# Rounding the experts' hidden layer: VectorE or ScalarE, with a second buffer

## The reference

```python
x = x + 0.5 * ffn(layernorm(x))
x = x + attn(layernorm(x))
x = x + 0.5 * ffn(layernorm(x))
```

## Time and profile before

| | |
|---|---|
| median of 3 runs | 596.25 us |
| the profiled execution | 595.64 us |
| its span, first to last instruction | 593.8 us |
| TensorE busy | 523.8 us (88%) |
| VectorE busy | 424.1 us (71%) |
| ScalarE busy | 215.2 us (36%) |
| GpSimd busy | 138.3 us (23%) |
| mean granted TensorE clock | 0.968 of full speed |

### The profile page before, as it was taken

One profiled execution on the slowest core, in us unless ns is written; L12 is line 12 of the kernel. 1 busy time (PEld: TensorE's weight loads), 2 busy tenths in 40 slices (PEclk: granted clock), 3 DMA queues, 4 the chain that ended last, 5 costly groups with the idle time before them and its releaser, 6 DMA issues.

```text
span 593.8 us, 7881 instructions
## 1 busy us (share of the span) xinstructions
PE 523.8 (88%) x2796; PEld 378.9 (64%) x2820; DVE 424.1 (71%) x796; ACT 215.2 (36%) x351; POOL 138.3 (23%) x131
## 2 busy tenths in 40 slices
PE   0485879999999999999999999999999656799997
PEld 0483556666676666758666676766667653577776
DVE  3759886986975686697476688735785777997742
ACT  0125633432624222271422254232221026665540
POOL 3140012354001324401323410132330100321220
PEclk9995989999999999999999999999999996999999
DMA  8995004000101000000200001030117940013112
GB/s 280 372 413 227 1 1 161 1 1 0 36 18 55 35 1 1 1 37 18 88 0 0 0 0 53 1 124 1 54 54 286 383 171 11 1 54 124 37 54 88
DMA packets 16607, 48.14 MB, mean 81 GB/s; under 512 B 1600, under 2 KB 1856, under 8 KB 15296
## 3 DMA queue, kind: packets, MB, share of 16 engines
q1 hardware_dynamic: 15760, 47.19, 21.3%
q10 hardware_dynamic: 816, 0.54, 0.5%
HBM read 39.33 MB, written 8.39 MB: 80 GB/s over the span
## 4 chain that ended last, share of the span: by engine, by line
PE 58%; DVE 15%; issue 13%; POOL 5%; DMA 3%; SPq 3%; ACT 2%; DVEq 0%; ACTq 0%; POOLq 0%
PE bank L382 8%; PE bank L635 8%; PE bank L642 8%; PE bank L384 8%; PE bank L383 8%; PE bank L636 7%; DMA route_w<-in_switch_w 3%; POOL rs L998 3%; SPq L408 2%; PE bank L600 2%; DVE h_lo L1194 2%; PE bank L514 2%; PE bank L486 1%; PE bank L532 1%; DVE h_hi L1193 1%
## 5 line engine op out<-in xcount | busy, mean ns | idle before, releaser
L635 PE MATMUL bank<-xh,win_hi 128*128 128x512 f32 x304 | 136.7, 450 | 0.0
L636 PE MATMUL bank<-xl,win_hi 128*128 128x512 f32 x304 | 119.5, 393 | 0.0
L642 PE MATMUL bank<-xbf,win_lo 128*128 128x512 bf16 x296 | 79.6, 384 | 1.7 <-issue 0.2
L998 POOL TENSOR_TENSOR rs<-ms,neg_half 128x16 f32<-128x16 f32 x16 | 49.2, 3077 | 129.0 <-ACT ms L843 129.0
L635 PEld LDWEIGHTS bank<-xh,win_hi 128*128 128x128 f32 x304 | 57.5, 189 | 17.4 <-issue 0.3
L636 PEld LDWEIGHTS bank<-xl,win_hi 128*128 128x128 f32 x304 | 57.3, 189 | 10.5
L985 POOL TENSOR_TENSOR xa<-xa,b_half 128x512 f32<-128x512 f32 x28 | 40.1, 1446 | 64.5 <-DVE z_lo L1212 32.1
L382 PE MATMUL bank<-w_hi,z_hi 128*128 128x512 f32 x128 | 51.6, 403 | 0.0
L642 PEld LDWEIGHTS bank<-xbf,win_lo 128*128 128x128 bf16 x320 | 25.0, 98 | 41.3 <-issue 22.7
L384 PE MATMUL bank<-w_hi,z_lo 128*128 128x512 f32 x128 | 50.0, 391 | 0.0
L383 PE MATMUL bank<-w_lo,z_hi 128*128 128x512 f32 x128 | 49.9, 390 | 0.0
(11 more groups left out here) (175 smaller groups left out, 1045.3 us busy)
## 6 DMA issues: line engine op xcount, KB each, us to landing
route_w<-in_switch_w SPq DMA_DIRECT2D x4, 2048.0 KB, 14.2
route_w<-in_switch_w SPq DMA_DIRECT2D x16, 512.0 KB, 16.3
raw<-in_w_in SPq DMA_DIRECT2D x4, 1280.0 KB, 18.7
xa<-in_x SPq DMA_DIRECT2D x4, 1024.0 KB, 6.6
out<-x SPq DMA_DIRECT2D x16, 256.0 KB, 2.0
x_dram<-x1p SPq DMA_DIRECT2D x12, 256.0 KB, 2.0
xa<-x_dram SPq DMA_DIRECT2D x3, 1024.0 KB, 5.6
x_chunk<-in_x SPq DMA_DIRECT2D x2, 1024.0 KB, 23.4
```

The source lines that it names most:

```text
L635: pe.matmul(bank[:], win_hi[:, c, r, k, :], xh[:, k, :], start=(k == 0), stop=False)
L636: pe.matmul(bank[:], win_hi[:, c, r, k, :], xl[:, k, :], start=False, stop=False)
L642: mm = pe.matmul(bank[:], win_lo[:, c, r, k, :], xbf[:, k, :], start=False, stop=(k == KC - 1))
L998: pool.tensor_tensor(rs[:], ms[:], neg_half[:], ALU.pow).then_inc(s_rs, 1)
```

## The change

The row ends (feed-forwards 1 to 3) get a second pair `h_hi2`, `h_lo2` for odd chunks. It lies in memory over `decay`, `qt`, `q_sq` and `yt`, which the attention is done with by then; the first write to it waits for the last y_lo. A chunk's rounding now waits for the O two chunks back. ScalarE rounds expert 0, between the two GELUs, and VectorE rounds expert 1. In phase 0 ScalarE rounds both experts, still with one pair, so that it waits for the O just before; for chunk 0 it waits for VectorE's second `select`. VectorE's split of w3 moves from between the splits of chunks 0 and 1 to behind `z_split(0, 0)`. TensorE's order and the late phase stay.

```diff
+        with ExitStack() as region:
+            h_hi2 = sb("h_hi2", [P, TOPK, S], F32R, into=region)
+            h_lo2 = sb("h_lo2", [P, TOPK, S], F32R, into=region)
         decay = sb("decay", [P, S])
...
+        hid2 = (hf, h_hi2, h_lo2)
...
         def hid_set(f, c):
-            return hid1 if is_late(f) and c % 2 else hid0
+            if is_late(f):
+                return hid1 if c % 2 else hid0
+
+            return hid0 if is_first(f) or c % 2 == 0 else hid2
...
+        def hid_reader(f, c):
+
+            if is_first(f):
+                return job_first(f"O{c - 1}") if c >= 1 else None
+            return job_row(f - 1, f"O{c - 2}") if c >= 2 else None
...
+            def hidden_act(f, c):
+
+                _, hi, _ = hid_set(f, c)
+                for k in range(TOPK):
+                    gelu(f, c, (k,))
+                    if k == 0 or is_first(f):
+                        reader = hid_reader(f, c)
+                        if reader is not None:
+                            act.wait_ge(s_ob, reader + 1)
+                        elif c == 1:
+                            act.wait_ge(s_yl, KC * f)
+                        else:
+                            act.wait_ge(s_sel[1], f + 1)
+                        act.wait_ge(s_gelu, H_JOBS * f + TOPK * c + k + 1)
+                        act.activation(hi[:, k, :], hf[:, k, :], ACT.Copy).then_inc(s_hh0, 1)
...
-                gelu(f, 0)
+                hidden_act(f, 0)
                 t1_out(f, 3)
-                gelu(f, 1)
+                hidden_act(f, 1)
                 for c in range(KC):
                     z_out(f, c)
                     if c < 2:
-                        gelu(f, c + 2)
+                        hidden_act(f, c + 2)
...
-                gelu(0, 0)
-                gelu(0, 1)
+                hidden_act(0, 0)
+                hidden_act(0, 1)
...
-            def split_hidden(f, c, read_job):
+            def split_hidden(f, c):
 
                 src, hi, lo = hid_set(f, c)
                 for k in range(TOPK):
-                    ve.wait_ge(s_gelu, H_JOBS * f + TOPK * c + k + 1)
-                    if k == 0 and read_job is not None:
-                        ve.wait_ge(s_ob, read_job + 1)
-                    own.do(ve.tensor_copy(hi[:, k, :], src[:, k, :]))
+                    if k == 0 or is_first(f):
+                        ve.wait_ge(s_hh0, hi_count(f, c, k))
+                    else:
+                        ve.wait_ge(s_gelu, H_JOBS * f + TOPK * c + k + 1)
+                        reader = hid_reader(f, c)
+                        if reader is not None:
+                            ve.wait_ge(s_ob, reader + 1)
+                        own.do(ve.tensor_copy(hi[:, k, :], src[:, k, :]))
                     ve.tensor_tensor(lo[:, k, :], src[:, k, :], hi[:, k, :], ALU.subtract).then_inc(s_hl, 1)
...
-            split_hidden(0, 0, None)
-            ve.wait_ge(s_w3h, 1)
-            ve.scalar_tensor_tensor(out=w3_lo[:], in0=w3_raw[:], scalar=0.5, in1=w3_hi[:], op0=ALU.mult,
-                                    op1=ALU.subtract).then_inc(s_w3l, 1)
+            split_hidden(0, 0)
             for c in range(KC):
-                job = job_first(f"O{c}")
                 if c < KC - 1:
-                    split_hidden(0, c + 1, job)
+                    split_hidden(0, c + 1)
                 z_split(0, c, x_bank[c])
+                if c == 0:
+                    ve.wait_ge(s_w3h, 1)
+                    ve.scalar_tensor_tensor(out=w3_lo[:], in0=w3_raw[:], scalar=0.5, in1=w3_hi[:], op0=ALU.mult,
+                                            op1=ALU.subtract).then_inc(s_w3l, 1)
```

More of the change, by code:

```diff
@@ L222, in macaron_kernel, with is_first @@
         hid1 = (hf1, h_hi1, h_lo1)
+        hid2 = (hf, h_hi2, h_lo2)
         first_chunk = [xa, x1p, x_chunk2, x_chunk3]
+        def is_first(f):
+            return isinstance(f, int) and f == 0
         def is_late(f):
@@ L293, in macaron_kernel @@
         s_hh = sem("s_hh")
+        s_hh0 = sem("s_hh0")
         s_hl = sem("s_hl")
@@ L360, in job_ffn, with hi_count @@
             return job_first(name) if isinstance(f, int) and f == 0 else job_row(f - 1, name)
+        def hid_reader(f, c):
+            if is_first(f):
+                return job_first(f"O{c - 1}") if c >= 1 else None
+            return job_row(f - 1, f"O{c - 2}") if c >= 2 else None
+        def hi_count(f, c, k):
+            return PAIR * c + k + 1 if is_first(f) else H_JOBS + KC * (f - 1) + c + 1
         def job_late(f, name):
@@ L772, in t1_out, with gelu @@
                 act.activation(use["xt_hi"][:, c, :], x_bank[c][:], ACT.Copy).then_inc(s_t1e, 1)
-            def gelu(f, c):
+            def gelu(f, c, ks=range(TOPK)):
                 if c == 0:
                     act.wait_ge(s_b1, f + 1)
-                for k in range(TOPK):
+                for k in ks:
                     act.wait_ge(s_h, H_JOBS * f + TOPK * c + k + 1)
@@ L890, in first_ffn @@
                     if c < 2:
-                        gelu(0, c + 2)
+                        hidden_act(0, c + 2)
             table_loads()
@@ L1351, in row @@
                         if n < KC - 1:
-                            split_hidden(b + 1, n + 1, job)
+                            split_hidden(b + 1, n + 1)
                         if n == 0:
@@ L1363, in row @@
                         if n == 0:
-                            split_hidden(b + 1, 0, None)
+                            split_hidden(b + 1, 0)
                         if n == 1:
@@ L1427, in _ @@
                 w3_add(2 * B - 1, t, job_late(2 * B - 1, f"W{t}"), out_bank(f"W{t}"))
-VE_ROW_STEPS = 60
+VE_ROW_STEPS = 56
 def kernel(**inputs):
```

## The result

The changed kernel took 598.87 us (median of 7 runs, 598.75 to 603.93), the kernel before in the same session 595.72 us. The ratio is 1.0066, 95% interval 1.0049 to 1.0083: slower, by 3.15 us in the medians where 2.5 was forecast. The profiled execution took 598.80 us. First its page: the span, the busy shares and the chain by engine.

A forecast was written before the change was run, and what follows sets the result against it. VectorE's load was taken as the main limit in the row ends, with ScalarE's copy late instead after the change. Phase 0 +3.1 and rows -0.6 give +2.5 on 596.25: 598.8 us, eight in ten runs from 596.9 to 601.3.

The forecast's parts named there:

- Likeliest case: Whole kernel: phase 0 costs +3.1 us, row ends give -0.6, so slower by 2.5 at 598.8 us; chance 0.56.
- step O1 to O2: Phase 0, step (5): from O1's end to O2's end takes 3.90 us, where it was 3.34, +0.56.
- step O2 to O3: Phase 0, step (6): from O2's end to O3's takes 3.68 us, where it was 3.34, +0.34.
- split of w3 moved: Phase 0: VectorE's split in its new place delays h_lo of (2,0) and O2; cost 0.15 us, bounds 0 and 1.05.
- own wait of ScalarE: Row ends: ScalarE's copy waits for its own preceding GELU, taken as 0.05 us, ends 0 and 0.17.
- gain per row end: Row ends: O2's last matmul starts at 265.41 instead of 265.61, -0.2 us each, -0.6 for three.
- (1): Phase 0: copy of (0,0) waits for VectorE's second select, GELU (0,1) queues behind; `hidden` 1 at 55.05 instead of 53.21, +1.84.
- (3): Phase 0: copy of (1,0) waits for O0 and holds up GELU (1,1); `hidden` 2 at 60.80 instead of 57.86.
- Relief whole: Rival for the row ends: copy off the path, VectorE's 1.84 us per row end won in full; 593.9 us, chance 0.05.
- Absorbed: Rival: a later wait shrinks by half of phase 0's delay or more; 595.7 to 597.2 us, chance 0.14.
- Dear own wait: Rival: ScalarE's own wait is 0.17, rows give +0.5 and phase 0 +0.6; 600.5 us, chance 0.07.
- Late clock: Rival in phase 0: idle gap behind O0, `hidden` 2 and O1 run at low clock, 1.8 us more; 600.6, chance 0.18.

The follow-up runs named there:

- experiment 1: Only the row ends changed against the kernel before (second buffer pair, ScalarE rounds expert 0 between the GELUs), phase 0 as before: 595.28 us, ratio 0.9991.
- experiment 4: Against experiment 1, ScalarE rounds expert 1 behind its GELU and VectorE expert 0 in the row ends: 591.41 us, ratio 0.9927.
- Experiment 8: Against experiment 1, ScalarE's copy of expert 0 stands behind both GELUs in the row ends: 595.23 us, ratio 0.9992.
- experiment 12: Against Experiment 8, VectorE and TensorE take expert 1 first in the row ends, GELUs wait in that order: 593.69 us, ratio 0.9974.
- experiment 5: Against the changed kernel, two buffer pairs in phase 0 too, odd chunks' pair where the routing weights were: 595.50 us, ratio 0.9999.
- experiment 11: Against experiment 5, even chunks take the pair where the routing weights were, so the first copy skips the select wait: 594.05 us, ratio 0.9967.
- its control: The changed kernel run again without any edit: 599.64 us over 6 runs, ratio 1.0089.
- experiment 6: Against experiment 4, phase 0 also gets two buffer pairs with ScalarE rounding expert 1 there: 589.76 us, ratio 0.9896.
- experiment 2: Only phase 0 changed against the kernel before (ScalarE rounds both experts, one pair, split of w3 moved), row ends as before: 599.42 us, ratio 1.0086.
- experiment 7: Against the changed kernel, VectorE's split of w3 is back between the splits of chunks 0 and 1: 597.68 us, a single execution.
- Experiment 9: Against the changed kernel, three extra unread matmuls on TensorE behind O0 of phase 0 fill its gap: 599.19 us over 6 runs.

## Why the prediction was right, step by step

**Likeliest case.** Slower was right, and so was the mechanism, in phase 0 and in the rows. That 598.87 fits 598.8 so closely is luck: the base of 596.25, a median of three, lay 0.53 above the 595.72 of seven, and the step was 0.65 larger than forecast (3.15 against 2.5). In the step one term was too large by 0.15, the rows gave 0.1 less, and one of +0.9 was missing.

| step | forecast | measured |
|---|---|---|
| phase 0: `hidden` 1 | 55.05 | 55.13 |
| end of O0 | 59.45 | 59.44 |
| `hidden` 2 | 60.80 | 60.83 |
| step O1 to O2 | 3.90 | 3.94 |
| step O2 to O3 | 3.68 | 3.72 |
| split of w3 moved | +0.15 | 0 |
| O3's end | 71.1 | 71.03 |
| row end: own wait of ScalarE | 0.05 | 0.09 |
| row end: GELU 1's end to `hidden` | 0.1 | 0.05 |
| `hidden` to `hidden` | 3.05 | 3.04 (row 0: 3.10) |
| gain per row end | 0.2 | 0, 0.25, 0.25 |
| late phase | nothing | +0.9 |

**The decision that carried it** was that `hidden` waits for both GELUs and the copy stands ahead of the second. The traces show it directly: `hidden` 1, 2 and 3 of the changed rows all wait for a GELU that stands behind a copy, the last two 3.04 us behind the one before. Experiments 1 and 4 differ only in the expert that ScalarE rounds: the first gives -0.4 us, the second -4.2. That is not the place of the copy alone. Experiment 8 moves only the place and gains nothing, as VectorE's order becomes the limit; experiment 12 mends that order and gains 0.2 to 0.3 per row. So the copy's place was the limit that stood in front, with a second one close behind, and the rival in which a copy off the path is worth 1.84 us per row had its condition too simple.

**The rows' bounds.** The 3.04 hides two terms off in opposite ways, the own wait and the release of TensorE (table). Row 0 gained nothing, and the prediction's reading that rows 0 and 2 repeat row 1 within 0.1 is wrong for row 0: before, its `hidden` 1, 2, 3 followed at steps of 2.99, 3.04, 2.99 (row 1: 2.86, 3.39, 2.74). In the changed kernel its `hidden` 1 follows `hidden` 0 by 3.74 (row 1: 3.58), and two steps of 3.10 and 3.11 follow. Its first expert-0 GELU follows `hidden` 1 by 0.97, but the copy starts 0.10 and `hidden` 0.15 behind what they wait for.

**Phase 0.** Steps (1) and (3) are confirmed by taking each away: without the wait for O(c-1) O3 ends 3.1 earlier (experiment 5), and without the select wait as well `hidden` 1 starts another 1.17 earlier and O3 ends another 0.8 earlier (experiment 11). The term of phase 0 that was mis-sized is the split of w3: h_lo of (2,0) did start at 64.9, 0.9 later than it could have, but O2 is held by its `hidden` until 65.65 and VectorE's first subtract is over by then.

**What was missing.** The delays of phase 0 and the gains of the rows leave row 2's `hidden` 0 at 355.60 instead of 353.00, +2.6, and its end at +2.35. The span grew by 3.2. The rest is in the late phase, where no instruction was changed. From its first `hidden` to its seventh it takes 28.50 us (494.14 to 522.64), before 27.58 (491.85 to 519.43): +0.92. All of that lies between the fourth and the fifth (506.52 to 512.16, 5.64 us; before 4.72), where TensorE waits for VectorE's z_lo. Timelines of VectorE, GpSimd and TensorE in that step, in the kernel before and in the changed kernel:

```profile
503.44 1.28 DVE L1200 TENSOR_TENSOR h_lo<-hf,h_hi 128x512 fp32r<-128x512 f32 x2
503.60 2.94 POOL L985 TENSOR_TENSOR xa<-xa,b_half 128x512 f32<-128x512 f32 x1 [24.91 <-DVE z_lo L1212]
508.19 0.66 PE L514 MATMUL bank<-ident_r,xnw 128*128 128x128 f32 x4 [1.40 <-DVE z_lo L1212]
```

```profile
505.74 2.38 DVE L1241 TENSOR_TENSOR h_lo<-hf,h_hi 128x512 fp32r<-128x512 f32 x2
505.89 1.69 POOL L1022 TENSOR_TENSOR xa<-xa,b_half 128x512 f32<-128x512 f32 x1 [24.91 <-DVE z_lo L1253]
511.41 0.66 PE L535 MATMUL bank<-ident_r,xnw 128*128 128x128 f32 x4 [2.26 <-DVE z_lo L1253]
```

The same two subtracts of VectorE take 2.38 us instead of 1.28, and GpSimd's add beside them 1.69 instead of 2.94; VectorE wins back 0.2 in a later operation. Which of the two gives way goes with the point where the clock rises. Windows of the kernel before and of the changed kernel, columns as in the earlier trace rows:

```profile
500.00:502.00 2.00, 2.00 (x12) 1.25 (x11) 2.00 (x5) 1.71 (x4) 0.00 (x0) 1.00 0.01 4
```

```profile
500.00:502.00 2.00, 2.00 (x6) 1.49 (x5) 0.33 (x1) 1.79 (x4) 0.00 (x0) 0.50 0.01 4
...
514.00:516.00 2.00, 2.00 (x6) 1.23 (x4) 1.83 (x6) 1.30 (x3) 0.00 (x0) 0.50 0.00 0
```

The granted clock rises at 499.6 before and at 502.8 in the changed kernel, 7.7 and 8.7 us behind the late phase's first `hidden`. Of the 14 profiled executions, the eight with a rise 7.7 to 8.5 us behind it have the short pair (1.28) and 27.58 to 27.80 us for the stretch; the five with 8.6 to 8.9 (the changed kernel, its control, experiments 1, 6 and 11) have the long pair (2.38 or 2.39) and 28.50 to 28.64. Experiment 8, with 10.5, takes 28.67 in another pattern. The second low stretch of the clock, which the changed kernel has from 513.0, is not the cause: it begins behind the fifth `hidden` (512.16), and experiments 2, 4, 5, 7, 9 and 12 have one too, at 27.63 to 27.80. Why the later rise turns the two engines' order isn't shown. The term belongs to an execution more than to the edit, since these instructions are the same in all of them; how often each kernel meets it isn't shown. It is also what experiment 6 misses (28.64). The sum is then phase 0 +2.9 (as row 0 sees it), rows -0.5, late phase +0.9: 3.3, beside 3.2 in the span.

**Rivals.** Relief whole: no for the change, though an order that was not mine to assume makes 1.3 of the 1.84 us real. Absorbed: no (experiment 2). Dear own wait: 0.09, nearer to 0.05 than to 0.17. Late clock: not in the profiled execution, where the granted clock rises shortly after 59 as before (0.97 from 59 to 60, before 0.87), ahead of the gap, which begins with O0's end at 59.44. It may be the executions near 604, whose mean clock is the lowest; they cost 5 us, more than the 1.8 I gave it, so the single late rise can't be all of it. Experiment 9's profile shows a second fall before O3's last matmul, a candidate for the rest. That stays open.

## What to carry to other kernels

Before moving an operation to an idle engine, look at what is queued behind it there and who waits for that: here 0.63 us of work on an engine 36% busy took the place of the bound it should have removed. Of several equal operations give away the one whose input comes last and whose result is used last, so that both engines start at once and neither waits for the other's order; the row ends with expert 1 for expert 0 gave -4.2 us instead of -0.4, and with expert 0's copy merely moved out of the way still -0.4. And where an engine takes over a wait (a buffer's reader, a select), the wait stops all of its queue: either a second buffer goes with it or the wait stays where it was hidden.

## What the runs showed of the hardware

An activation that waits for its own predecessor on ScalarE starts 0.09 us behind its recorded end (258.67 to 258.76), where two independent ones overlap by 0.11; such a wait costs 0.2 us. Where VectorE's subtracts and GpSimd's add of 128x512 ran side by side in the late phase, one gave way to the other: the two subtracts took 1.28 us beside an add of 2.94, or 2.38 beside an add of 1.69 (another add of that kind, at 508.21 in the kernel before, took 1.28). The Trainium skill ("TensorE: Matmul & The Clock Gate", Part 1) says that the point of the clock's rise moves from run to run because its activity window runs freely; the traces agree that it moves: in the late phase, whose instructions are the same in all kernels here, the granted clock rises 7.7 to 8.9 us behind the first `hidden` in 13 profiles and 10.5 behind it in one. With the rise the same stretch took 27.58 to 28.67 us. In a kernel whose TensorE idles in pieces, such a term of about 1 us stands beside every sum made from one profile.
